# Layer 3's sums in three pairs of PSUM banks, one one-hot instruction for four columns of the sort, and chunks of 16 slots in layers 0 and 2

## The reference

```python
h = (x @ W.T).reshape(N, H, C)                        # layer 0: H = 4 heads of C = 64
a_s, a_d = einsum(h, att_src), einsum(h, att_dst)
e = leaky_relu(a_s[src] + a_d[dst], 0.2)              # one score for an edge and head
m = segment_max(e, dst)                               # softmax over the edges of a node
p = exp(e - m[dst])
alpha = p / (segment_sum(p, dst)[dst] + 1e-16)
out = segment_sum(alpha[:, :, None] * h[src], dst)    # weighted sum of the neighbours
out = elu(out + bias) + x

# layer 1: 8 heads of 32; exp(alpha - its maximum over all edges), no bias, no elu
# layer 2: 4 heads, edges grouped by src instead of dst, the score times edge_weight, relu
# layer 3: layernorm with gamma and beta, then two attentions side by side
#          (4 heads of 64, 8 heads of 32), elu, and (512 x 256) @ Wu + bu
```

## Time and profile before

| | us |
|---|---|
| median of 3 runs | 4878.01 |
| lowest and highest | 4874.40, 4884.42 |
| time of the profiled execution | 4869.96 |
| its span, first to last instruction | 4868.2 |

### The profile page before, as it was taken

How to read it: one execution, slowest core, us unless ns; L and a number is a source line. 1 busy time by engine, 2 the same in 40 slices (tenths; PEclk the granted TensorE clock), 3 DMA queues, 4 the chain that set the end, 5 groups by cost and what they waited for, 6 DMA issues and landing times. The chain is left out here.

```text
span 4868.2 us, 74715 instructions
## 1 busy us (share of the span) xinstructions
PE 3104.0 (64%) x14124; PEld 2235.3 (46%) x14204; DVE 3152.1 (65%) x10653; ACT 2250.4 (46%) x8908; POOL 2855.3 (59%) x2739
## 2 busy tenths in 40 slices
PE   1577875777623666645777773566662677777776
PEld 0366664656422444433545542344431355555554
DVE  5887775666454555574767764666664577777776
ACT  0355554555422333334666663333334355555454
POOL 0377776777706777724777752777750465555522
PEclk9855556555556777766666676767775799898899
DMA  1000000000024444424555532444440666666531
GB/s 50 1 2 2 2 2 2 2 2 2 2 56 135 128 133 132 127 35 118 139 143 139 144 86 87 132 132 121 131 79 13 213 187 173 173 173 171 167 92 61
DMA packets 235833, 449.02 MB, mean 92 GB/s; under 512 B 80264, under 2 KB 132390, under 8 KB 235110
## 3 DMA queue, kind: packets, MB, share of 16 engines
q0 software_dynamic: 130816, 317.16, 25.2%
q1 hardware_dynamic: 104752, 128.89, 8.1%
HBM read 416.04 MB, written 29.80 MB: 92 GB/s over the span
## 5 line engine op out<-in xcount | busy, mean ns | idle before, releaser
L1237 POOL DMA_INDIRECT rows.4<-feats,by_dst_other.1 x464 | 511.5, 1102 | 564.8 <-issue 342.1
L1237 POOL DMA_INDIRECT rows.2<-feats,by_dst_other.1 x464 | 494.5, 1066 | 279.6 <-POOLq L976 138.5
L1237 POOL DMA_INDIRECT rows.1<-feats,by_dst_other.1 x464 | 490.8, 1058 | 280.5 <-POOLq L976 139.4
L1237 POOL DMA_INDIRECT rows.3<-feats,by_src_other.1 x448 | 475.5, 1061 | 255.8 <-issue 128.3
L658 POOL DMA_INDIRECT by_dst_records<-r_rec.1,r_idx.1 x448 | 443.2, 989 | 161.1 <-issue 127.9
L658 POOL DMA_INDIRECT by_src_records<-r_rec.2,r_idx.2 x416 | 413.5, 994 | 143.7 <-issue 112.3
L1445 ACT ACTIVATE rows.4<-rows.4,xres.1 128x65 f32<-128x65 f32 x1856 | 448.0, 335 | 0.9
L1364 PE MATMUL m_p.4<-rows.4,xres.1 128*128 128x264 f32 x1044 | 324.0, 438 | 145.7 <-DVE acc.4 L1613 109.8
L1445 ACT ACTIVATE rows.2<-rows.2,e_prob.2 128x33 f32<-128x33 f32 x1856 | 397.9, 315 | 0.0
L1613 DVE TENSOR_TENSOR acc.4<-acc.4,m_p.4 128x264 f32 x522 | 200.4, 425 | 219.3 <-PE m_p.4 L1381 183.6
L1345 PE MATMUL m_p.3<-rows.3,m_oh.3 128*128 128x260 f32 x896 | 309.2, 497 | 16.4 <-DVE rows.3 L1594 15.5
(11 more groups left out here) (761 smaller groups left out, 8230.6 us busy)
## 6 DMA issues: line engine op xcount, KB each, us to landing
e_line.1<-by_dst_own_row SPq DMA_DIRECT2D x29, 512.0 KB, 4.7
e_line.2<-by_dst_own_row SPq DMA_DIRECT2D x29, 512.0 KB, 4.4
e_line.4<-by_dst_own_row SPq DMA_DIRECT2D x58, 256.0 KB, 5.0
e_line.3<-by_src_own_row SPq DMA_DIRECT2D x28, 512.0 KB, 4.6
xres.1<-by_dst_masks SPq DMA_DIRECT2D x232, 48.0 KB
e_mask.2<-by_dst_masks SPq DMA_DIRECT2D x29, 320.0 KB
rows.1<-feats,by_dst_other.1 POOLq DMA_INDIRECT x464
rows.2<-feats,by_dst_other.1 POOLq DMA_INDIRECT x464
```

The costliest lines, as they stand in the source:

```text
L1237: pool.indirect_dma_start(out=rows[:, s % RING, :], out_offset=None, in_=feats, in_offset=bass.IndirectOffsetOnAxis(ap=g.other[:, s:s + 1] ...
```

## The change

Three parts:

1. **Sort.** A bf16 copy `k_lob` of `k_lo` is made, and the four `tensor_scalar` compares of a batch (128 x 128 each) become one `tensor_tensor` compare of 128 x 512, in the histograms and in both `place_edges`.
2. **Chunks.** CS is 16 in all layers, so layers 0 and 2 go through 29 and 28 chunks (15 and 14 before), and their chain is laid as in layer 1.
3. **Layer 3's banks.** BANKS is 3 (six banks). `e_pc` is put into free columns of `e_pt`'s bank, and `e_po` is cut to one bank: a slot's own scores take 2 x 12 columns for 3 x 12, and the third part is added in PSUM by a second matmul for each slot. `opening` waits once, for both attentions' adds of group g - 3. `closing` signals once, and DVE adds a group by one instruction of 2 x 264 columns. ACT's `factors` waits for `shifted`, so it comes behind DVE's `shift`.

```diff
-        for j in range(B):
-            dve.tensor_scalar(self.ohlo[:, par, j, :], iotab[:, :], g.k_lo[:, bass.ds(n * B + j, 1)], None, ALU.is_equal)
+        dve.tensor_tensor(self.ohlo[:, par, :, :], iotab[:, :].unsqueeze(1).to_broadcast([P, B, P]),
+                          g.k_lob[:, bass.ds(n * B, B)].unsqueeze(2).to_broadcast([P, B, P]), ALU.is_equal)
...
-    CS = 32 if HS == 4 else 16
+    CS = 16
...
-    STEP = 512 * FOLDS // CS
+    STEP = 512 // CS
...
-    BANKS = 4 // NC
+    BANKS = 4 if NC == 1 else 3
+    PARTS = 3 if NC == 1 else 2
...
-                    ins = pe.matmul(po[:, s - s0, 0:3 * HS], hot[:, hh % 2, i * P:(i + 1) * P],
-                                    parts[:, :, bass.ds(ids[s % 4], 1), :].rearrange("p k a h -> p k (a h)"), start=True, stop=True)
+                    own_hot = hot[:, hh % 2, i * P:(i + 1) * P]
+                    ins = pe.matmul(po[:, s - s0, 0:PARTS * HS], own_hot,
+                                    parts[:, 0:PARTS, bass.ds(ids[s % 4], 1), :].rearrange("p k a h -> p k (a h)"), start=True, stop=PARTS == 3)
+                    if PARTS == 2:
+                        ins = pe.matmul(po[:, s - s0, HS:2 * HS], own_hot,
+                                        parts[:, 2, bass.ds(ids[s % 4], 1), :].rearrange("p a h -> p (a h)"), start=False, stop=True)
...
                 scaled(s)
+                if group >= BANKS:
+                    pe.wait_ge(S["added"].sem, S["added"].at(group_added(group - BANKS)))
                 for k in range(NC):
-                    if group >= BANKS:
-                        pe.wait_ge(S["added"].sem, S["added"].at(group_added(group - BANKS) - NC + 1 + k))
...
-                for k in range(NC):
-                    a = acc[:, bass.ds(tile, 1), k * AW:(k + 1) * AW].rearrange("p a f -> p (a f)")
-                    dve.tensor_tensor(a, a, pp[:, group % BANKS, k, 0:AW], ALU.add).then_inc(S["added"].sem, 1)
+                a = acc[:, bass.ds(tile, 1), :].rearrange("p a (k f) -> p (a k) f", k=NC)
+                dve.tensor_tensor(a, a, pp[:, group % BANKS, :, 0:AW], ALU.add).then_inc(S["added"].sem, 1)
```

More of the change, by code:

```diff
@@ L615, in onehots @@
                     dve.wait_ge(S["counts"].sem, S["counts"].at(-1) + n)
-                for j in range(B):
-                    dve.tensor_scalar(ohlo[:, quarter % 2, j, :], iotab[:, :], g.k_lo[:, bass.ds(n * B + j, 1)], None, ALU.is_equal)
+                dve.tensor_tensor(ohlo[:, quarter % 2, :, :], iotab[:, :].unsqueeze(1).to_broadcast([P, B, P]),
+                                  g.k_lob[:, bass.ds(n * B, B)].unsqueeze(2).to_broadcast([P, B, P]), ALU.is_equal)
                 dve.tensor_tensor(ohhi[:, quarter % 2, :, :], iota_row[:, 0:T].unsqueeze(1).to_broadcast([P, B, T]),
@@ L1162, in group_added @@
     def group_added(k):
-        return (k + 1 + k // (CS // 2 + 1)) * NC
+        return k + 1 + (k // (CS // 2 + 1)) * NC
     def halves(c):
@@ L1380, in closing @@
                 for k in range(NC):
-                    pe.matmul(pp[:, group % BANKS, k, 0:1], zeros[:, :], zeros[:, 0:1], start=False, stop=True).then_inc(S["closed"].sem, 1)
+                    ins = pe.matmul(pp[:, group % BANKS, k, 0:1], zeros[:, :], zeros[:, 0:1], start=False, stop=True)
+                ins.then_inc(S["closed"].sem, 1)
             turns = (turn_scores, turn_ends, turn_carry, turn_back)
```

25 lines of the change are left out of this document (15 added, 10 removed).

## The result

| | us |
|---|---|
| before, median of 8 | 4876.43 |
| changed, median of 8 | 4847.66 (4826.27 to 4858.62) |
| ratio | 0.9938, 95% interval 0.9923 to 0.9953 |
| forecast | 4848, 4795 to 4915 |

The changed kernel is 28.8 us faster; the forecast was 30 to 31. The number is right, but partly by luck: a stage that the prediction had at nothing lost 22 us, and the term for layer 3 was too small by some 25. The two errors nearly cancel, and that is the main thing to learn here. The profiled span is 4841.2 us, 27.0 less than before.

A forecast was written before the change was run, and what follows sets the result against it. It took POOL's issue to bound the first placing and layers 0 to 2, DVE the histogram, and the PE-DVE loop layer 3. Terms -6 - 5 - 8 - 12 = -31 from the median 4878.01 gave 4847, stated as 4848, range 4795 to 4915.

The forecast's parts named there:

- the term for layer 3: Layer 3: three edits together save 0.4 us a chunk, -12 us in all, from -70 to +45.
- Sort, histogram: First histogram on DVE: the merged compare takes 0.59 us for 0.65 a batch; -6 us, bounds 0 to -37.
- rival D: Sort: the merged compare runs at two elements a cycle, 31 us more gain, 4817 us; chance 0.05.
- in both placings the gain lands behind POOL: Both placings: DVE has slack and POOL sets the time, so the faster compare gives 0 there.
- if the placings change: Sign against the forecast: POOL's DMAs in the placings were to keep 989 ns and their pace.
- Layers 0 and 2: Chunks of 16 shorten the tails while POOL's streams stay at 631 and 611 us: -5 and -8 us.
- Rival C: Layers 0 and 2: chunks of 16 make DVE the bound; +11 us in all, 4889 us; chance 0.08.
- the price of the picks: Layer 3, PE: doubled picks add 3.2 us of sequencer time a chunk, of which 1.9 counts on the path.
- the removed waits: Layer 3: PE's waits for a bank until DVE's adds are done, 3.6 to 3.8 us a chunk, go.
- The walk: Layer 3: one chunk stepped through from `score` to `score`, 28.5 us for 29.1 before; 0.4 a chunk was taken.
- Rival A: Layer 3: the bank waits go whole, -2.5 us a chunk; -91 us in all, 4787 us; chance 0.17.
- Rival B: Layer 3: picks' sequencer time and low clock outweigh removed waits, +1.5 us a chunk; 4902 us in all; chance 0.17.

The follow-up runs named there:

- only_sort: The kernel before with part 1 alone, the merged compare in both histograms and both placings: 4900.92 us, ratio 1.0043.
- h2_single: The changed kernel with four `tensor_scalar` compares again in the histogram beside the first placing: 4824.65 us, ratio to before 0.9898.
- h2_tt128: The changed kernel with the compare in the histogram beside the first placing as four `tensor_tensor` of 128 x 128: 4823.12 us, ratio to before 0.9897.
- h2_psum: The changed kernel with the merged compare beside the first placing reading its constant row from PSUM: 4817.26 us, ratio to before 0.9887.
- split_scale: `h2_psum` with chunks of 32 again in layers 0 and 2, and DVE's row multiplication in layers 0 to 2 halved: 4818.44 us, ratio to before 0.9884.
- only_chunks: The kernel before with part 2 alone, chunks of 16 slots in layers 0 and 2: 4872.91 us, ratio 0.9993.

## Why the prediction was right, and where it wasn't

**Sort, histogram: right.** -6 forecast, -7.6 in the balance. The merged compare takes 681 ns for 512 columns, as the 682 ns float row had it. The rule cited from the Trainium skill, "VectorE: DVE Perf Modes", agrees, and rival D is out: the batch is at 0.78, not 0.5. The saving was read from one batch of 0.82 us; the mean was 0.86.

**Sort, placing: wrong, 0 forecast, +22.2 measured.** The step that failed is "in both placings the gain lands behind POOL". It asked only whether POOL would wait for DVE's indices, and that stayed as it was (32.6 us for 33.3). It took the length of POOL's own instruction as given. By the prediction's own sign ("if the placings change") its mechanism is wrong here. `only_sort` and `h2_single` put the loss on the histogram's compare beside it, `h2_tt128` and `h2_psum` on its two SBUF sources held for 0.68 us. The sign of it was in rows that I had: the gathers of the earlier trace rows have a median of 1019 ns and a maximum of 1545 in the kernel before, and nothing in the prediction asked what lengthens them. That the total was met all the same is luck.

**Layers 0 and 2: small terms, half right.** -5 forecast for layer 0, +3.9 - 7.7 = -3.8 by the balance; -8 for layer 2, +6.3 - 10.5 = -4.2. The tails came nearly as forecast: 36.1 us for 44.1 in layer 0 (37 forecast), 44.1 for 55.5 in layer 2 (43 to 48). The loops didn't stay at 631 and 611. Rival C gave the symptom (a longer loop) to a DVE that is the bound; the whole growth is in the length of POOL's gathers, so it is again DVE's instructions in POOL's way. That `scale` is one of them `split_scale` shows; which instructions of the chain add to it wasn't tested. By `only_chunks` the whole part is within the noise.

**Layer 3: right in sign, three times too small.** -12 forecast, -36 alone, -39 in the balance (29.5 and 9.7). The step that failed is the price of the picks, 1.9 us a chunk, set against the removed waits (3.6) as if the two were independent; beside it the merged add was put at nothing. With two pairs the picks cost 2.6. With three the words of picks take no longer than before (2.19 us in the mean both times), because the second of them runs ahead; one further matmul for a slot costs 1.0. The merged add gives 0.5. The walk took every pick at the sequencer's pace and had no place for the second word. The forecast of the net was -0.4 us a chunk, measured is -1.2. Rival A (-2.5) is further off on the other side; half of the removed waits came back at the turns, for which it had no place. Rival B's premises came true (more low clock, 0.87 for 0.90; picks at the sequencer's pace in one word) and its conclusion didn't, because the other word's picks became nearly free. A chunk of before was taken at 30.55 or 31.2 us; over all `score` rows it is 30.75.

**The sum.** -31 forecast, -28.8 measured, by +22 that was missed and some -25 that was underrated. That they nearly cancel is luck. Either error alone would have moved the time to 4870 or 4823, both still within the wide range.

## What to carry to other kernels

Where POOL issues indirect DMAs back to back, look at the spread of their length, not at their median, and keep DVE's instructions with two SBUF sources short, or give them one source in PSUM; look at long `tensor_scalar` instructions with a source in SBUF as well. A merge that saves DVE time can cost the engine beside it more. A buffer that removes a wait on an in-order engine may also free its sequencer, so price it together with the register work that stands behind the wait.
